# Top-32 mask by a second exponential on ScalarE and a subtraction on GpSimd, with new orders of work and a later load of Wq

## What is computed

```
x = x + attention(layernorm(x), ctx)          # q, k with axial rope, softmax, @ Wout + bout
y = layernorm(x); xn = y * rsqrt(mean(y*y) + eps) * norm_w
logits = xn @ Wc.T / clip(temperature, 0.1)   # (128, 1024) for a tile
top_vals, top_idx = top_k(logits, 32)
expressed = softmax(top_vals) @ genes[top_idx]
x = x + tanh(expressed @ Wd.T) * xn * (expressed @ Wu.T) * scale
```

## Time and profile before

| | us |
|---|---|
| median of 3 runs | 482.34 |
| lowest and highest run | 481.61, 484.61 |
| the profiled execution, its own time | 482.9 |
| its span, first to last instruction | 481.1 |
| granted TensorE clock, mean | 0.972 of full |

### The profile page before, as it was taken

The page is one execution under the profiler, slowest core; times in us unless marked ns, Lnnn a source line. Parts: engine busy times, 40 slices in busy tenths (PEclk is TensorE's granted clock), DMA queues, the critical chain, the costliest instruction groups (busy, mean ns, idle before and its releaser), DMA issues.

```text
span 481.1 us, 11034 instructions
## 1 busy us (share of the span) xinstructions
PE 424.9 (88%) x3898; PEld 326.1 (68%) x3898; DVE 383.8 (80%) x616; ACT 279.2 (58%) x420; POOL 264.6 (55%) x258
## 2 busy tenths in 40 slices
PE   2849789999999999999999989999999989999734
PEld 1637567677777777777777777777777767777522
DVE  3985176479899979797979799797979898999980
ACT  3683764657467757576757566675747565643421
POOL 1416795647279757575757676574747362204322
PEclk9997899999999999999999999999999999999985
DMA  7853604424042422406060605042230504100000
GB/s 249 254 118 134 91 14 89 101 53 91 8 101 40 93 55 51 94 14 129 12 131 12 131 1 120 22 91 52 52 91 17 106 3 89 46 3 22 22 22 23
DMA packets 80989, 34.23 MB, mean 71 GB/s; under 512 B 72112, under 2 KB 74176, under 8 KB 80960
## 3 DMA queue, kind: packets, MB, share of 16 engines
q1 hardware_dynamic: 79856, 32.53, 29.3%
q10 hardware_dynamic: 1104, 1.31, 0.9%
HBM read 12.60 MB, written 4.19 MB: 35 GB/s over the span
## 4 chain that ended last, share of the span: by engine, by line
PE 54%; DVE 12%; SPq 11%; issue 9%; DMA 8%; ACT 4%; POOL 1%; DVEq 0%; POOLq 0%; ACTq 0%
PE psum L1607 30%; SPq L348 8%; DMA x_ring<-x_dram 4%; PE psum L1736 3%; DVE row_max L1204 3%; PE psum L1828 3%; PE psum L1771 3%; PE psum L1847 3%; PE psum L1761 2%; DVE stage_a L1275 2%; DMA qT<-parts 2%; DVE top L1266 2%; PE psum L1699 2%; SPq L293 2%; DMA stage_b<-L_xattn_Wkv_dram 2%
## 5 line engine op out<-in xcount | busy, mean ns | idle before, releaser
L1204 DVE TENSOR_REDUCE row_max<-psum 128x8 f32<-128x1024 f32 x64 | 74.6, 1218 | 12.6 <-PE psum L1699 12.5
L1266 DVE MAX8 top<-stage_a 128x8 f32<-128x1024 f32 x64 | 78.1, 1220 | 2.3 <-ACT stage_a L785 1.3
L1275 DVE MATCH_REPLACE8 stage_a<-top,stage_a 128x1024 f32<-128x1024 f32 x64 | 77.3, 1207 | 0.0
L462 POOL TENSOR_TENSOR qk_cos<-stage_b,cos_t 128x512 f32<-128x512 f32 x31 | 39.8, 1284 | 57.3 <-issue 44.4
L749 ACT ACTIVATE stage_b<-psum 128x1024 f32<-128x1024 f32 x64 | 64.0, 1029 | 10.4 <-PE psum L1736 10.0
L508 POOL TENSOR_TENSOR stage_c<-stage_c 128x512 f32<-128x512 f32 x16 | 20.6, 1287 | 63.6 <-ACT stage_c L814 63.6
L1607 PE MATMUL psum<-wcT_h,yT_h 128*128 128x512 f32 x128 | 51.0, 398 | 0.7 <-ACT stage_b L755 0.4
L1607 PE MATMUL psum<-wcT_l,yT_h 128*128 128x512 f32 x128 | 50.8, 397 | 0.0
L1607 PE MATMUL psum<-wcT_h,yT_l 128*128 128x512 f32 x128 | 50.3, 393 | 0.0
L463 POOL TENSOR_TENSOR qk_sin<-stage_b,sin_t 128x512 f32<-128x512 f32 x31 | 43.5, 1402 | 0.0
L483 POOL TENSOR_TENSOR parts<-turned,parts 128x512 f16<-128x512 f32 x31 | 36.1, 1170 | 12.5 <-issue 9.6
(11 more groups left out here) (137 smaller groups left out, 1090.5 us busy)
## 6 DMA issues: line engine op xcount, KB each, us to landing
out_dram<-x_ring SPq DMA_DIRECT2D x16, 256.0 KB, 2.8
x_ring<-x_dram SPq DMA_DIRECT2D x15, 256.0 KB, 2.8
ctx_sb<-ctx_dram SPq DMA_DIRECT2D x16, 128.0 KB, 2.1
stage_a<-L_ffn_Wc_dram SPq DMA_DIRECT2D x1, 2048.0 KB, 12.3
stage_b<-L_xattn_Wq_dram ACTq DMA_DIRECT2D x1, 1024.0 KB, 7.2
stage_b<-L_xattn_Wkv_dram SPq DMA_DIRECT2D x2, 512.0 KB, 8.9
stage_c<-L_xattn_Wout_dram SPq DMA_DIRECT2D x1, 1024.0 KB, 5.9
qT<-neg_maxT SPq DMA_DIRECT2D x32, 8.0 KB
```

The lines of the kernel that those rows point to most:

```text
L462: pool.tensor_tensor(halves(qk_cos), halves(qk_sb), trig(cos_t, t), ALU.mult).then_inc(s_cosm[n], 1)
L1204: nc.vector.tensor_reduce(row_max[:, 0:HEADS].rearrange("p (odd m) -> p odd m", odd=2)[:, :, 4 * g:4 * g + 4], score_of[g][:].rearrange("p ...
L1266: nc.vector.max(top[:, 8 * n:8 * n + 8], logit if n == 0 else rest).then_inc(s_top[n], 1)
L1275: nc.vector.match_replace(rest, top[:, 8 * n:8 * n + 8], logit if n == 0 else rest, REMOVED).then_inc(s_rem[n], 1)
```

## The change

`mask` leaves VectorE. Its product is replaced by three steps. ScalarE takes the exponential of `rest` with the same bias (`exp_rest`): the removed elements give zero, the others the same values as in `gene_w`. GpSimd subtracts the two rows of 1024 (`mask`, now in GpSimd's list), which leaves the top 32 and exact zeros. The sum of the row comes from a third ScalarE instruction over the 32 values in `top` (`sum_top`), and VectorE keeps only the reciprocal of it (`invert_sum`). `find_top(t, 0)` and `negate_top` get waits for the new readers of `top`, `rest` and `neg_top`.

The load of Wq on ScalarE's queue now stands behind the small constants and a wait for x of tile 0.

All lists of all engines are new, and with them the bank tables and the waits that guard the banks. The loop has the same number of iterations, but its body is cut at another point: some steps that ran in iteration i now run in the next one, or the other way round.

```diff
+            def mask(t):
+                pool.wait_ge(s_rexp, t + 1)
+                pool.wait_ge(s_gexp, t + 1)
+                pool.tensor_tensor(gene_w, gene_w, rest, ALU.subtract).then_inc(s_gw, 1)
...
+            def sum_top(t):
+                act.wait_ge(s_top[3], t + 1)
+                act.wait_ge(s_ntop, t + 1)
+                if not first(t):
+                    act.wait_ge(s_ginv, t)
+                nc.scalar.activation(top_exp[:], top[:], ACT.Exp, bias=neg_top[:],
+                                     accum_out=gene_sum[:]).then_inc(s_tsum, 1)
+
+            def exp_rest(t):
+                act.wait_ge(s_rem[3], t + 1)
+                act.wait_ge(s_ntop, t + 1)
+                nc.scalar.activation(rest, rest, ACT.Exp, bias=neg_top[:]).then_inc(s_rexp, 1)
...
-            def mask(t):
-                dve.wait_ge(s_rem[3], t + 1)
-                dve.wait_ge(s_gexp, t + 1)
-                nc.vector.scalar_tensor_tensor(gene_w, rest, REMOVED, gene_w, ALU.is_equal, ALU.mult,
-                                               accum_out=gene_sum[:]).then_inc(s_gw, 1)
-                dve.wait_ge(s_gw, t + 1)
+            def invert_sum(t):
+                dve.wait_ge(s_tsum, t + 1)
...
             act.dma_start(slot(0), x[0]).then_inc(s_x, 16)
-            act.dma_start(wq_raw, wq.rearrange("(k p) n -> p k n", p=P)).then_inc(s_wq, 16)
             act.dma_start(norm_sb[:], norm_w).then_inc(s_small, 16)
...
+            act.wait_ge(s_x, 16)
+            act.dma_start(wq_raw, wq.rearrange("(k p) n -> p k n", p=P)).then_inc(s_wq, 16)
...
             def logits(t, n):
...
                 elif n == 1:
                     pe.wait_ge(s_yT_l, t + 1)
+                    if later(t, 1) and upto(t, 13):
+                        pe.wait_ge(s_ex[3], t + 3)
...
                 transpose_o(15)
                 express(12)
+                transpose_attn(15)
                 transpose_y(14)
-                transpose_attn(15)
+                down_up(12, 0)
                 down_up(12, 1)
-                down_up(12, 0)
+                project_out(15)
+                logits(14, 1)
                 logits(14, 0)
-                logits(14, 1)
-                project_out(15)
```

1115 lines of the change are left out of this document (575 added, 540 removed).

## The result

The changed kernel takes 498.22 us (median of 4 runs, 494.57 to 499.44), the kernel before 482.97 beside it (4 runs). The ratio is 1.0302, with a 95% interval of 1.0248 to 1.0356. The forecast was 475.9, range 470 to 483: wrong in sign.

A forecast was written before the change was run, and what follows sets the result against it. PE was taken to bound the loop, its idle time caused by a late VectorE. Loop -6.4, start -0.7, drain -1.7 and tail +2.4 gave -6.4 us, from the median of 482.34 to 475.9; range 470 to 483, at 0.80.

The forecast's parts named there:

- What bounds the kernel: Loop: PE sets the pace, busy 200.05 of 208 us; its idle time comes from VectorE, late for x.
- first rival: Loop: PE finds all its idle time, the loop gives 9.2 us and the time is 473; chance 0.10.
- The loop, minus 6.4: Eight iterations: 9.2 us of PE's waits won, less 2.8 for a new wait at the second half of the logits.
- the wait of 2.67 us should be gone: Loop: VectorE's wait for x before the statistics vanishes, since x is issued earlier, between the two `turn`s.
- second rival: Loop: k's transpose lands late and replaces x's wait; iteration stays 26.0 us, time 481 to 482.3; chance 0.18.
- The wait for `exp_group(i-3, 3)`: Loop: PE waits 0.35 us at `logits(i-5, 1)` for this exponential, costing 2.8 us over 8 iterations.
- The start, minus 0.7: Up to the first exponentials: scores(0) start 0.7 us later, but transposed scores come sooner; 0.7 us won.
- The drain, minus 1.7: After the loop: VectorE drops work worth 1.3, 1.7 and 0.7 us, loses 2.0 waiting for `find_top(15, 0)`; 1.7 won.
- The tail, plus 2.4: End: nothing hides the last mask, 3.7 us from last removal to PE in place of 1.3.
- third rival: Loop and drain: mask late for PE's `transpose_w`, a microsecond each time costs 13 us, time 489; chance 0.12.
- The fourth: Loop: GpSimd's subtraction and VectorE's search take turns, PE loses 11 us over the forecast, time 487; chance 0.06.
- my bound of 1.8 us lost: Start: the worse bound, where the whole delay of q(0) from Wq's later load passes through; 1.8 us lost.

The follow-up runs named there:

- b1: Kernel before with its own orders, only the new mask used for every tile: 486.39 us, ratio 1.0068.
- b3: Kernel before with its own orders, new mask only for tiles 2 to 9, VectorE's mask for the others: 474.16 us, ratio 0.9804.
- a8: Changed kernel; in the loop SP issues q's transpose, x, k's transpose, then the context: 490.10 us, ratio 1.0168.
- a7: Changed kernel; in the filling Wout's low part later, tile 2's norm power ahead of k's rope, first exponentials in PE's order: 494.21 us, ratio 1.0253.
- b5: Kernel before; tile 2's `project_k` moved behind the transpose of tile 1's row maxima, k's read and split following: 490.94 us, ratio 1.0176.
- b8: Kernel before with new mask for tiles 2 to 14, own buffer for the new exponential, Wout's low part sooner: 480.36 us, ratio 0.9957.
- b2: Kernel before; only Wq's load issued behind a wait for x of tile 0: 488.27 us, ratio 1.0101.
- a1: Changed kernel; only Wq's load issued at once, second on ScalarE's queue: 497.59 us, ratio 1.0297.
- a9: Changed kernel; in the loop PE takes the third group of values ahead of the next tile's first scores: 496.42 us, ratio 1.0294.
- a6: Changed kernel; in the loop SP issues x first, then both transposes back to back, then the context: 500.93 us, ratio 1.0378.

## Why the prediction was wrong, step by step

**What bounds the kernel** held. PE sets the loop's pace, VectorE was late for x, and its mask was the last thing ahead of the maxima: with the mask gone and nothing else moved (b1, b3) an iteration falls by 1.04 to 1.10 us, near the 1.15 of the first rival.

**The loop, minus 6.4: failed; -0.8 in eight iterations.** The step that failed is "the wait of 2.67 us should be gone": x's wait is still 14.0 us. In the loop the second rival is what happened, and I had given it 0.18. It had the mechanism and the place; the term that was off is "context and x with the gaps of SP some 0.9" us: they took 2.1. With that, and q's transpose 0.4 us later than walked, k's goes out at 6.3 us after `values(i-3, 0)` (200.64) instead of 4.7. PE wants the keys at 10.2 (10.1 by my walk) and takes them at 11.4, 5.2 us after the issue for the 4.5 that I had booked. What no rival had is that x was late as well. Moving the context behind k's transpose (a8) gives an iteration of 25.1 us, for the forecast's 25.2. The wait for `exp_group(i-3, 3)` that I priced at 0.35 doesn't show in the list of waits.

**The start, minus 0.7: failed, and with it the largest part.** I costed the start up to the first exponentials and took everything from there to tile 7 as unchanged. scores(0) started at 42.30, not 36 to 38: `project_q(1)`, for which I had booked 2.8 us, took 5.4 (36.92 to 42.30) at a granted clock of 0.50 (35 to 40 us). Tile 0's shift is still only 1.8 later, within the scatter. The 9.3 us from tile 0 to tile 5, where the loop begins, had no term in my sum at all. I had seen only that `project_v(1)` stands behind the values, and booked it as "still to be done". What the runs name in that stretch: the subtraction for Wout beside GpSimd's power with the order of the exponentials (about 2 by the traces, a7). The late k of tile 2 isn't shown as a cause (b5). How the rest, some 7 us, divides stays open; the traces point at two projections ahead of tile 1's transposed scores and at the lower clock.

**The drain, minus 1.7: not seen in the time, plus 2.5** (2.1 between tile 13 and 15, and 2.8 behind, less the tail's 2.4). But I had said that PE leaves the loop with about 2.4 us less done and that this cancels; by this cut it doesn't, since those matmuls lie in the drain of one kernel and ahead of it in the other. PE's idle time from tile 13 to the end grew by 0.7, which is -1.7 + 2.4 of my sum. The agreement is partly luck, because the matmuls of the end also ran at a lower clock, 0.84 for 0.88. VectorE's idle time ahead of `find_top(15, 0)`, forecast near 2, was 2.47.

**The tail, plus 2.4: right**, 3.7 us for 1.3. So were the subtraction's 2.4 us and the exponential's 1.16.

**The third rival** (mask late at `transpose_w`) didn't come in the loop, but it did in the drain of b1 and b8. **The fourth** is out: with the new mask and the old orders PE is never idle in the loop, and the search's instructions keep their length. I weighed the port for the new mask alone, and it bit elsewhere, in a step that had only been moved. The Trainium skill ("SBUF — State Buffer", "Who interferes with whom") has that rule: a VectorE instruction with two SBUF inputs contends with a GpSimd instruction that reads SBUF, and the port pair they share is an exclusive lock. The trace agrees: the power ends at 52.33, 0.4 us after the subtraction (51.92).

**Wq's load:** my bound of 1.8 us lost was too low for the old order (5, b2) and too high for the new one (0.6, a1).

## What to carry to other kernels

When a change brings new orders, price every stretch of the program, the filling too: the stretch that I had taken as unchanged lost 9.3 us, more than the 6.4 forecast for the loop, and this pipeline gave back nothing of what was lost ahead of it (b2, b5). Compare PE's idle time beside the lengths of stretches, because a new order moves work over the cuts. Before trusting that a wait goes away, add up everything its queue issues ahead of it, gaps included, and look for a second transfer that is late behind the same one: a9 freed one of two and won nothing, a8 moved what delayed both. And separate the edit from the orders: the new mask was worth 8 us (b3) where VectorE had been late and its result had slack (the loop of the old orders), and cost time where PE took it at once (the drain, the tail).

## What the runs showed of the hardware that I had not expected

SP's queue is slower than its rows look. Between the end of one transpose's issue (204.81) and the start of the next (206.91) two loads with rows of 0.81 and 0.34 us took 2.1. And a load can wait for a store that was issued just ahead of it, though nothing in its own row says so (a6).

VectorE and GpSimd took turns for one instruction of 2048 columns with two inputs from SBUF, whichever came first:

```profile
69.29 2.28 DVE L1161 TENSOR_TENSOR wout_l<-stage_c,wout_h 128x2048 fp32r<-128x2048 f32 x1
69.32 3.40 POOL L463 TENSOR_TENSOR qk_sin<-stage_b,sin_t 128x512 f32<-128x512 f32 x1
```

```profile
67.81 3.34 DVE L1187 TENSOR_TENSOR wout_l<-stage_c,wout_h 128x2048 fp32r<-128x2048 f32 x1
...
68.97 3.33 POOL L453 TENSOR_TENSOR x_ring<-x_ring,bout_sb 128x512 f32<-128x512 f32 x1
```

The first pair is from the kernel before: VectorE came first, 2.28, and GpSimd's product took 3.40, its own 1.29 and about the whole of the other. The second is from b3: GpSimd was at work, VectorE took 3.34, and the next GpSimd instruction 3.33. A line's duration in the profile holds that waiting, and no row calls it idle.
